# State-space stage: tokens taken in blocks of runs of 32, and u projected by four 128x32 matmuls side by side

## What is computed

```
x      = x + ssm(layernorm(x))
proj   = x @ in_proj_w;  hidden, gate = split(proj)            # 1024 channels each
u      = silu(conv4(hidden))
dt,B,C = split(u @ x_proj_w, [128, 16, 16]), each rms-normed    # 160 columns
dt     = softplus(dt @ dt_proj_w + dt_proj_b)
s_t    = exp(dt_t * A) * s_{t-1} + (dt_t * u_t) * B_t           # 16 states per channel
y_t    = sum_n s_t[n] * C_t[n] + u_t * D
out    = (y * silu(gate)) @ out_proj_w
```

## Time and profile before

| | us | share of the span |
|---|---|---|
| median of the three runs | 5462.37 | |
| the profiled execution, its own time | 5468.6 | |
| its span, first to last instruction | 5466.8 | |
| PE (TensorE matmuls), busy | 4975.0 | 91% |
| DVE (VectorE), busy | 4462.5 | 82% |
| POOL (GpSimd), busy | 3175.6 | 58% |
| ACT (ScalarE), busy | 2636.9 | 48% |

### The profile page before, as it was taken

One profiled execution on the slowest core, in us unless ns is written; L12 is line 12 of the kernel. 1 busy time (PEld: TensorE's weight loads), 2 busy tenths in 40 slices (PEclk: granted clock), 3 DMA queues, 4 the chain that ended last, 5 costly groups with the idle time before them and its releaser, 6 DMA issues. The chain is left out here.

```text
span 5466.8 us, 107541 instructions
## 1 busy us (share of the span) xinstructions
PE 4975.0 (91%) x41287; PEld 2967.0 (54%) x41287; DVE 4462.5 (82%) x7277; ACT 2636.9 (48%) x4245; POOL 3175.6 (58%) x1659
## 2 busy tenths in 40 slices
PE   6899999999999999999999999987499999999983
PEld 3345444444444444444444445443388888888863
DVE  3988889888898888889888898886578888888864
ACT  3555556555565655556555565552133333333320
POOL 1676766767667676666766667675144444444427
PEclk9999999999999999999999999998799999999975
DMA  2222212222122222222222222221300000000001
GB/s 83 82 88 81 102 65 101 92 80 101 71 101 80 91 92 75 99 79 93 99 73 100 80 86 97 74 94 68 127 25 27 27 27 27 27 27 27 27 13 2
DMA packets 114433, 384.29 MB, mean 70 GB/s; under 512 B 29184, under 2 KB 30720, under 8 KB 81024
## 3 DMA queue, kind: packets, MB, share of 16 engines
q1 hardware_dynamic: 101600, 373.47, 19.3%
q0 software_dynamic: 9216, 0.27, 0.5%
q10 hardware_dynamic: 3104, 3.58, 0.2%
HBM read 342.92 MB, written 34.34 MB: 69 GB/s over the span
## 5 line engine op out<-in xcount | busy, mean ns | idle before, releaser
L336 POOL TENSOR_TENSOR s<-s,Cb 128x1024 f32<-128x1024 f32 x1024 | 2394.9, 2361 | 1084.2 <-DVE state L657 1073.8
L652 DVE TENSOR_TENSOR_SCAN s<-s,state,BU 128x512 f32<-128x512 f32 x2048 | 2452.8, 1260 | 426.5 <-PE BU L738 393.4
L502 ACT ACTIVATE s<-dt,ch 128x512 f32<-128x512 f32 x2048 | 1305.5, 712 | 780.4 <-PE Y L755 779.0
L755 PE MATMUL Y<-s,ident 64*64 64x512 f32 x8192 | 1014.9, 611 | 76.2 <-POOL s L336 75.2
L684 PE MATMUL PJ<-xnT,w_in 128*128 128x512 f32 x2048 | 946.1, 606 | 9.3 <-ACT dtuT L368 5.7
L738 PEld LDWEIGHTS BU<-spread,dtuT 32*128 32x128 f32 x16384 | 513.3, 189 | 527.7 <-DVE s L652 399.3
L738 PE MATMUL BU<-spread,dtuT 32*128 32x128 f32 x16384 | 611.9, 286 | 144.0 <-DVE s L652 139.6
L684 PEld LDWEIGHTS PJ<-xnT,w_in 128*128 128x128 f32 x2048 | 369.7, 190 | 478.5 <-issue 423.4
L755 PEld LDWEIGHTS Y<-s,ident 64*64 64x64 f32 x8192 | 279.7, 134 | 573.6 <-issue 535.7
L729 PE MATMUL PJ<-w_out,u 128*128 128x512 f32 x1024 | 472.3, 605 | 8.2 <-ACT xnT L372 6.7
L729 PEld LDWEIGHTS PJ<-w_out,u 128*128 128x128 f32 x1024 | 184.9, 190 | 243.3 <-issue 225.5
(11 more groups left out here) (238 smaller groups left out, 7095.1 us busy)
## 6 DMA issues: line engine op xcount, KB each, us to landing
Cb<-bc SPq DMA_DIRECT2D x256, 1024.0 KB, 4.8
res<-in_x SPq DMA_DIRECT2D x64, 256.0 KB, 4.8
x<-res SPq DMA_DIRECT2D x64, 256.0 KB, 4.9
x1t<-x SPq DMA_DIRECT2D x64, 256.0 KB, 2.6
out<-r_t SPq DMA_DIRECT2D x64, 256.0 KB, 2.0
xt<-in_x SPq DMA_DIRECT2D x31, 512.0 KB, 5.7
w_in<-in_in_w SPq DMA_DIRECT2D x8, 512.0 KB, 9.6
x_all<-in_factors SPq DMA_DIRECT2D x4, 1024.0 KB, 5.1
```

What stands on the lines that cost most here:

```text
L336: nc.gpsimd.tensor_tensor(pair, pair, Cb[q % 2][:, 2 * part * T:2 * part * T + 2 * T], ALU.mult).then_inc(z_ready, 1)
L502: nc.scalar.activation(s[k % SLOTS][:, n, :], dt[p % 2][:, gi, :], ACT.Exp, scale=ch[:, 2 * p + gi, 7 + 4 * nq + n:8 + 4 * nq + n]).then_i ...
L652: nc.vector.tensor_tensor_scan(s[k % SLOTS][:, n, :], s[k % SLOTS][:, n, :], BU[:, n::4], state[:, b, k, n:n + 1], ALU.mult, ALU.add).then ...
L755: last_ = nc.tensor.matmul(Y[r][y_rows(r, gi), :], ident[rows, rows], s[(k_even + gi) % SLOTS][rows, n, :], start=False, stop=(n == 3 and ...
```

## The change

Block tb now holds the tokens 128i + 32tb + t, for i from 0 to 3 and t from 0 to 31: four runs of 32. In `x_proj` each matmul with 128 tokens becomes four with 32 tokens, one for each run, at the column positions 0, 32, 64 and 96 of the array, each with the same 160 columns of `w_xp`. `turned` writes runs of 32 in place of every fourth element. `dt_times_u` becomes two products of 128x512 that read dt and u in runs of 32 and write `dts` in block order, so that `turn_dtu` reads 128 neighbours. `b_product` writes 128 neighbouring columns of BU, where before it wrote four neighbours in every sixteen.

```diff
--- before.py
+++ after.py
@@ -186,8 +186,14 @@
             at = 64 * (gi if r == 0 else 1 - gi)
             return slice(at, at + 64)
 
-        def by_block(ap):
-            return ap.rearrange("p (q b) -> p b q", b=TB)
+        def block_of(ap, tb):
+            return ap[:, tb * P:(tb + 1) * P]
+
+        def blocks(ap):
+            return ap.rearrange("p (b i t) -> p b i t", b=TB, i=4)
+
+        def blocks_of_plain(ap):
+            return ap.rearrange("p (i b t) -> p b i t", b=TB, i=4)
 
         block = ctx.enter_context(nc.Block())
 
@@ -398,11 +404,11 @@
 
             def turned(ring_, period):
                 act.wait_ge(ring_.full, ring_.filled(("turn", 0), period))
-                nc.scalar.copy(by_block(dtnT[:]), PJ[ring_.bank(("turn", 0))][:].rearrange(
-                    "p (b q) -> p b q", b=TB)).then_inc(ring_.taken["act"], 1)
+                nc.scalar.copy(blocks_of_plain(dtnT[:]), blocks(PJ[ring_.bank(("turn", 0))][:])
+                               ).then_inc(ring_.taken["act"], 1)
                 act.wait_ge(ring_.full, ring_.filled(("turn", 1), period))
-                nc.scalar.copy(by_block(cT), PJ[ring_.bank(("turn", 1))][0:NSTATE, :].rearrange(
-                    "p (b q) -> p b q", b=TB)).then_inc(ring_.taken["act"], 1)
+                nc.scalar.copy(blocks_of_plain(cT), blocks(PJ[ring_.bank(("turn", 1))][0:NSTATE, :])
+                               ).then_inc(ring_.taken["act"], 1)
 
             def dt_bias(ring_, p, period):
                 for gi in range(2):
@@ -582,8 +588,10 @@
             def dt_times_u(p, n, c_of, slot):
                 dve.wait_ge(u_ready, 2 * (c_of + 1))
                 dve.wait_ge(dt_ready, n + 1)
-                nc.vector.tensor_tensor(dts[:], dt[p % 2][:], u[slot][:, 2 * p:2 * p + 2, :], ALU.mult
-                                        ).then_inc(dtu_ready, 1)
+                for gi in range(2):
+                    last_ = nc.vector.tensor_tensor(blocks(dts[:, gi, :]), blocks_of_plain(dt[p % 2][:, gi, :]),
+                                                    blocks_of_plain(u[slot][:, 2 * p + gi, :]), ALU.mult)
+                last_.then_inc(dtu_ready, 1)
 
             def add_res(ring_, j, period, c_prev):
                 dve.wait_ge(ring_.full, ring_.filled(("out", j), period))
@@ -692,8 +700,11 @@
                     bank_of(ring_, use, period)
                 bank = PJ[ring_.bank(use)]
                 for g in range(G):
-                    last_ = nc.tensor.matmul(bank[:, tb % 2 * SP_:(tb % 2 + 1) * SP_], by_block(u[slot][:, g, :])[:, tb],
-                                             w_xp[:, g, :], start=(g == 0), stop=(g == G - 1))
+                    for i in range(4):
+                        at = P * i + 32 * tb
+                        last_ = nc.tensor.matmul(bank[32 * i:32 * i + 32, tb % 2 * SP_:(tb % 2 + 1) * SP_],
+                                                 u[slot][:, g, at:at + 32], w_xp[:, g, :],
+                                                 start=(g == 0), stop=(g == G - 1), tile_position=(0, 32 * i))
                 if tb % 2 == 1:
                     last_.then_inc(ring_.full, 1)
 
@@ -721,7 +732,7 @@
                 for gi in range(2):
                     bank = bank_of(ring_, (f"tr{p}", gi), period)
                     for tb in range(TB):
-                        last_ = nc.tensor.transpose(bank[:, tb * P:(tb + 1) * P], by_block(dts[:, gi, :])[:, tb], ident[:])
+                        last_ = nc.tensor.transpose(bank[:, tb * P:(tb + 1) * P], block_of(dts[:, gi, :], tb), ident[:])
                     last_.then_inc(ring_.full, 1)
 
             def out_proj(bank, j, part, slot):
@@ -735,7 +746,7 @@
                 for tb in range(TB):
                     for i in range(4):
                         rows = slice(32 * i, 32 * i + 32)
-                        last_ = nc.tensor.matmul(BU[:, i * T:(i + 1) * T].rearrange("p (t b n) -> p b t n", b=TB, n=4)[:, tb], dtuT[rows, gi, tb, :],
+                        last_ = nc.tensor.matmul(block_of(BU[:, i * T:(i + 1) * T], tb), dtuT[rows, gi, tb, :],
                                                  spread[rows, nq, tb].rearrange("p t n -> p (t n)"),
                                                  start=True, stop=True, tile_position=(32 * i, 0))
                 last_.then_inc(dbu_ready, 1)
```

## The result

The changed kernel takes 5394.18 us, the median of 4 runs between 5391.35 and 5396.23; the kernel before took 5463.69 beside it. The ratio is 0.9868, with a 95% interval from 0.9856 to 0.9881: 69.5 us, or 1.3%, faster. The forecast was 5381 with a range from 5360 to 5425. The range holds the time; the forecast's own range, 5372 to 5389, misses it by 5 us. The profiled execution has a span of 5394.4 us, 72.4 less than before.

The account below looks back on a forecast made before the run. TensorE and DVE were taken to alternate on the single BU, the strided projection load making DVE wait. Gains of 74.3 and 6.7 us (81.0), minus 1.9, plus 2.4, gave 81.5: median 5381 us, range 5360 to 5425.

Parts of the forecast that it names:

- the forecast's own range: Total time with each projection block at its bounds, a gain of 4.5 to 5.5 us a chunk: 5372 to 5389 us.
- The projection: In x_proj, four narrow records cost about one wide: a block 2.36 us instead of 3.96, two 4.60 instead of 7.69.
- The redone schedule of units 24 to 26: One chunk's BU starts come 1.11, 4.20 and 4.95 us earlier; DVE's waits become 1.19, 2.59 and 0.15 us.
- DVE would be next in line: Units 24 to 26: of 6.3 us TensorE saves a chunk, 1.3 turn into TensorE waiting for DVE.
- L1623: Attention-stage row of the same tile shape: 32 records in 1.01 us, 109 ns loads overlapping; taken as the projection's cost.
- a load overlaps only matmuls of another row group: Rule behind a rival: each narrow projection load waits for its rows' matmuls, 16.0 us a block, 6232 us; chance 0.02.
- `b_product`: Left at 1.10 us, no gain from neighbouring writes; a rival had up to another 26 us, 5355, chance 0.04.
- all that follows moves by the same 4.95: From unit 27 on, every piece waits for one that moved, so 15 chunks gain 4.95 us each, 74.3 us.
- the rival on instructions: TensorE's instructions arrive too slowly for 128 records and 128 loads in unit 24: 1.5 us a chunk, 5404; chance 0.05.
- the start: Ahead of chunk 0, four projection blocks in a row take 9.1 us instead of 15.8, a gain of 6.7 us.
- +0.06 a pair: The two products of dt_times_u cost 0.06 us more than one, counted in units 13 and 22: +1.9 us.
- the 190 of L684: Transposes of dts load neighbours in 190 ns instead of 210, counted in unit 31: -2.4 us over 15 chunks.

Follow-up runs that it names:

- wide_neighbours: The changed kernel with one full 128x128 load of 128 neighbouring tokens per projection matmul instead of four 128x32 ones, token order mixed up; 5389.08 us, ratio 0.9861.
- tiles_strided: The kernel before with only x_proj on four column tiles of 32 tokens, still reading every fourth float of u; 5397.25 us in one run.
- pad_32: The changed kernel with 32 unneeded identity matmuls (128 records) into BU ahead of everything; 5388.02 us in one run.
- pad_32_before: The kernel before with 32 unneeded identity matmuls into BU ahead of everything; 5477.00 us in one run.

## Why the prediction was right, and where it was not

**Right, term by term.** The projection: 2.36 us a block and 4.60 for two were put down; a block alone shows 2.38, two take 4.48 from start to next start (2101.78 - 2095.42 less 1.88 for the sum over states), and a chunk 9.44 busy. The redone schedule of units 24 to 26: 4.95 us a chunk forecast, 5.07 measured from unit 23 to 26, with the predicted waits within 0.12. That DVE would be next in line, and TensorE wait for it in units 24 and 26, shows in the brackets of 0.61 and 0.82. That L1623 was the row to go by is borne out: 4096 loads of 111 ns, 455 us if they stood in a row, lie within 151 us of matmuls. The rule of the Trainium skill, "TensorE: Matmul & The Clock Gate", Part 3, that a load overlaps only matmuls of another row group, does not hold for these tiles. `b_product` stayed at 1.17 us a burst with neighbours written. The Trainium skill, "Advanced Engine Details and Errata", PSUM Cachelines, states that any non-contiguous pattern slows matmuls; at runs of four floats these traces show no such slowing, 1.17 us either way.

**Wrong: "all that follows moves by the same 4.95".** This step held within a chunk and failed across the loop's branch. Five chunks gained 2.7 us each where the five between them gained 5.0, 11 us in all. I had looked at one chunk in the middle of an iteration, and the rows showed none that begins behind a branch; the rival on instructions placed the risk in unit 24, in the long burst, where nothing happened. It named the right cause (instructions that are not there in time) at the wrong place.

**Mis-sized: the start.** 6.7 us were put down ahead of chunk 0 and 4.4 came (first scans at 121.98 and 117.54 us). The durations were taken from stretches at full clock, and this one starts at half: the four blocks took 11.34 us, and 9.1 were put down.

**Mis-sized: dt_times_u.** +0.06 a pair was put down and 0.07 measured; the late start of unit 28 that its extra instructions brought, 0.35 us in twelve chunks or 4 us, was not in the sum. Against that stand gains that were not counted: the transposes load in 141 ns, not the 190 of L684. A nearer row stood in the trace of the kernel before, the transposes of x, which load 128 neighbours:

```profile
L677 PEld LDWEIGHTS PJ<-ident,xt 128*128 128x128 f32 x256 | 28.6, 146 | 49.2 <-issue 35.2 <-DVE xt L529 8.6 <-ACT dtuT L368 4.6
```

And ahead of the first unit 2.07 us are waited instead of 2.23; the 0.35 us in unit 6 of every second chunk, 2 us in all, went, and so did the stop of 0.50 us in unit 14 of the same chunks, up to 3 us.

**The account.** From the starts of the scans, the 72.4 us of the spans are 4.4 ahead of chunk 0, 13.6 in the five chunks that end in a branch, 52.6 in the other ten, 1.4 in the last chunk and 0.4 behind it. The forecast had 6.7, then 25.0 and 49.9, and nothing or a loss of 0.1 in the last. So the range holds the time because it left room for a stall in supply, and not because each term came out.

**Why the change works.** The explanation ahead of the prediction, that the strided load sets the pace, was right. But it named one way out, and there were two. The load can be made quicker (wide_neighbours, 154.0 us, a timing only, since that run mixes up the tokens; a correct kernel with wide loads of neighbours was not built) or be spread over column tiles that load side by side (tiles_strided, 151.3 us).

## What to carry to other kernels

In this kernel a stationary operand read with a stride of 16 bytes cost nothing once its matmuls were cut into column tiles and issued in turns (151.3 us against 151.1 with neighbours); issued tile by tile, 32-column matmuls cost three times as much. Matmuls added ahead of the loop moved the span by 8 us in either direction (pad_32 and pad_32_before): before crediting or blaming the edit, compare the chunks that begin behind the branch with the others, or write the loop out. Written out, this kernel with the change is 1.9% faster than before (5363.12 us), and the change alone is worth 81.9 us, close to what its schedule said.

## What was not expected of the hardware

- Loads of a column tile overlap the loads and matmuls of the other column tiles, though all use the same 128 rows: 111 ns each at one in 37 ns.
- Strided by 16 bytes, a load of 32 columns took 137 ns against 111, one of 128 columns 329 against 193.
- A pause of TensorE in the middle of a burst, 1.80 us at "issue", behind a loop's branch, that comes and goes with 16 or 32 matmuls added at the start of the program, and ends 1.2 to 1.6 us after a packet of 16384 bytes of instructions has come.
- Inside the loop DVE starts 0.35 us late at one fixed unit, and which unit depends on how many instructions DVE has in a chunk. With the loop written out, no unit that waits for BU is late in this way.
- The loop itself costs the kernel before 1.4 us in each chunk that no branch ends (230.2 against 228.8 us).
